# Five hand-written engine orders laid out anew, in an attention and feed-forward kernel for eight batches

## The chip, the cores and the metric

The kernel runs on one core of a Trainium2 chip. The core has a matrix engine (TensorE, PE in the rows), a vector engine (VectorE, DVE), a scalar engine (ScalarE, ACT), GpSimd (POOL) and SyncE (SP), which here only issues transfers. Each engine works through its own instructions in order, and waits on semaphores that the others and the transfers count up. The metric is the device time of one launch, in microseconds; lower is better.

## The reference

Eight batches of 512 tokens with 512 features go through two stages, each followed by a layer normalization whose result is added to the stage's input.

```python
x = x + layernorm(attn(layernorm(x)))        # 16 heads of 32, rotary positions, softmax, low-rank q and k/v (128)
x = x + layernorm(ffn(layernorm(x)))
# attn: q = rotary(c_q @ W_qr + b_qr), k = rotary(x @ W_kr + b_kr), v = c_kv @ W_uv + b_uv
#       c_q = x @ W_dq + b_dq, c_kv = x @ W_dkv + b_dkv
#       out = softmax(q k^T / sqrt(32)) v @ W_o + b_o
# ffn:  h = silu(x' @ W_gate.T * s_g) * (x' @ W_up.T * s_u);  y = fwht(h * SU_dp) @ W_down.T * s_d
#       x' = fwht(x * SU_ug); 2048 inner features
```

## The kernel before, in words

Every fp32 product is made of three fp16 products (high by high, high by low, low by high), so nearly every operand exists as a high and a low half. One batch is cut into steps, and a step is named by its kind and its number:

- `c.0`, `c.1`: the two compressions; `proj.g`: rotary inputs of head group g (4 heads of 4 groups); `v.0`, `v.1`: values. On TensorE `proj` is lines 764 and 772, `v` line 750, `c` line 738.
- `smax.g.n` (TensorE line 784, VectorE line 1326): the row maxima of group g, from scores that are made only for that; they go into `tok` (`mtok`) and then, by a transposing transfer `stq.g`, into the q stack. `stk.g.0` and `stk.g.1` (line 592) transpose the k and q stacks of group g before that; `smax.g.0` waits for both, the group's first `st` waits for `stq.g`.
- `st.U` (line 796), U = 0 to 31 in a batch, 8 for each group: one block of scores, transposed, 128 keys by 256 queries by 4 heads. ScalarE then does `exp.U` (line 1016), `exq.U` (1022) and `exr.U` (1027), VectorE `low.U` (1340, left half) and GpSimd `low.U` (1437, right half) make the low half of the probabilities `pr`.
- `av.U` (lines 812 and 817): the value product and the row sums of block U, 20 matmuls whose outputs are 32 partitions high, four of them side by side in the array. All other steps fill 128 columns of it. `pr` has two buffers, so `exp.U` waits for `av.(U-2)`; `av.U` waits for both `low.U`. After each fourth `av` a `norm.n` (VectorE, ScalarE, GpSimd) divides.
- `o.t`: output projection of 128 tokens (lines 826, 831), then normalizations `oe`, `ys`, `yn` and a transposing transfer `ln2.t` (line 570).
- `gate.i`, `up.i`, `down.i`, i = 0 to 31 (8 for each 128 tokens): the feed-forward products (lines 842, 842, 866). Between them stand `tanh.i`, `gelu.i`, `hid.i` on ScalarE, VectorE and GpSimd. `down.i` also waits for its weights, the transfer `wl.i` (line 548), which waits for `down.(i-2)`.
- `xs`, `xn`, `xl`, `ln1`: load, normalize and transpose the next batch's input. `oe.t` and `fe.t` on SP write the two results of 128 tokens; `rl` and `yl` load.

PSUM has two slots for `c`, `v`, `proj`, `smax`, `st` and `o`; the table `UPPER` says which step takes which. A step's matmuls wait for the slot's last user to be read out.

The order on each engine is written out as text, one string per engine: `FRONT` (executed once), `ORDER` (a hardware loop of six turns) and, after the loop, `ORDER` twice more with what lies beyond the last batch left out. The loop overlaps three batches: `up.4@-1` in turn b is the feed-forward step of batch b-1, `c.1@1` the one of batch b+1. `FRONT` also scales, splits and rotates the weights (`lda`, `amx`, `mx`, `ldx`, `cut`, `dy`, `dz`, `ut`, `uh`, with 56 `warm` matmuls between them to keep TensorE at work).

```python
steps(FRONT[name][skip:], FRONT_PRED)
with nc.Fori(1, NB - 1, engines=(eng.engine,), hint_back_edge=True) as b:
    steps([(b + d, s) for d, s in ORDER[name]], None)
steps(back(name), BACK_PRED)
```

Of the kernel before, what the change touches and what calls it, by code (L numbers as in the profile page):

```python
# [64 lines left out]
        smax.3.1 down.12@-1 up.15@-1 smax.3.2 c.1@1 smax.3.3 av.18 down.13@-1 av.19 st.20 c.0@1 gate.16@-1 down.14@-1
        smax.3.4 smax.3.5 up.16@-1 down.15@-1 st.21 proj.0@1 gate.17@-1 smax.3.6 up.17@-1 smax.3.7 gate.18@-1 av.20
        st.22 up.18@-1 av.21 gate.19@-1 down.16@-1 st.23 up.19@-1 down.17@-1 gate.20@-1 av.22 st.24 up.20@-1 av.23
        gate.21@-1 st.25 down.18@-1 up.21@-1 av.24 gate.22@-1 smax.0.0@1 down.19@-1 smax.0.1@1 av.25 st.26 up.22@-1
        smax.0.2@1 down.20@-1 gate.23@-1 smax.0.3@1 st.27 up.23@-1 smax.0.4@1 down.21@-1 av.26 smax.0.5@1 gate.24@-1
        av.27 st.28 proj.1@1 up.24@-1 st.29 down.22@-1 smax.0.6@1 gate.25@-1 av.28 smax.0.7@1 up.25@-1 st.30 av.29  # L70
        st.31 gate.26@-1 down.23@-1 up.26@-1 av.30 gate.27@-1 av.31 up.27@-1 v.0@1 gate.28@-1 st.0@1 down.24@-1
        up.28@-1 v.1@1 gate.29@-1 st.1@1 down.25@-1 o.0 av.0@1 down.26@-1 smax.1.0@1 av.1@1 up.29@-1 smax.1.1@1 st.2@1
        gate.30@-1 o.1 down.27@-1 smax.1.2@1 up.30@-1 av.2@1 gate.31@-1 st.3@1 o.2 down.28@-1 up.31@-1 smax.1.3@1
        down.29@-1 st.4@1 av.3@1 o.3 down.30@-1 smax.1.4@1 gate.0 down.31@-1 smax.1.5@1 proj.2@1 up.0 st.5@1 gate.1
# [5 lines left out]
        tanh.8@-1 exr.12 xn.0@1 hid.7@-1 exp.13 exq.13 tanh.9@-1 xn.1@1 exr.13 tk.3.0 norm.2 yl.1@-1 hid.8@-1 exp.14  # L80
        exq.14 hid.9@-1 fe.0@-1 tanh.10@-1 exr.14 tk.3.1 exp.15 tanh.11@-1 exq.15 hid.10@-1 exp.16 exr.15 xn.2@1
        exq.16 exr.16 hid.11@-1 exp.17 tanh.12@-1 exq.17 exr.17 hid.12@-1 xn.3@1 tanh.13@-1 exp.18 exq.18 exr.18
        exp.19 exq.19 hid.13@-1 exr.19 tanh.14@-1 hid.14@-1 c.1@1 norm.3 tanh.15@-1 exp.20 hid.15@-1 exq.20 c.0@1
        exr.20 tanh.16@-1 exp.21 hid.16@-1 exq.21 exr.21 tanh.17@-1 tk.0.0@1 exp.22 norm.4 fe.1@-1 tanh.18@-1
        hid.17@-1 exq.22 exr.22 exp.23 hid.18@-1 tanh.19@-1 exq.23 tk.0.1@1 exr.23 hid.19@-1 exp.24 exq.24 tanh.20@-1
        exr.24 exp.25 exq.25 fo.0@-1 exr.25 tanh.21@-1 hid.20@-1 exp.26 hid.21@-1 exq.26 tanh.22@-1 exr.26 norm.5
        exp.27 exq.27 hid.22@-1 exr.27 tanh.23@-1 hid.23@-1 yl.2@-1 exp.28 exq.28 exr.28 tanh.24@-1 exp.29 exq.29
        hid.24@-1 exr.29 norm.6 tanh.25@-1 exp.30 exq.30 exp.31 exr.30 exq.31 exr.31 hid.25@-1 tk.1.0@1 tanh.26@-1
        tanh.27@-1 fe.2@-1 v.0@1 exp.0@1 tk.1.1@1 exq.0@1 exr.0@1 v.1@1 norm.7 hid.26@-1 exp.1@1 exq.1@1 exr.1@1
        tanh.28@-1 oe.0 hid.27@-1 hid.28@-1 tanh.29@-1 exp.2@1 exq.2@1 exr.2@1 yn.0 oe.1 tanh.30@-1 exp.3@1 hid.29@-1  # L90
        exq.3@1 exr.3@1 oe.2 hid.30@-1 tanh.31@-1 exp.4@1 yl.3@-1 exq.4@1 hid.31@-1 exr.4@1 yn.1 oe.3 norm.0@1 fe.3@-1
        tanh.0 exp.5@1 exq.5@1 yn.2 exr.5@1 tanh.1 hid.0 tk.2.0@1 hid.1 exp.6@1 exq.6@1 exr.6@1 exp.7@1 exq.7@1 tanh.2
        yn.3 exr.7@1
# [1420 lines left out]
```

## Time and profile before

| | |
|---|---|
| Time, median of 3 runs | 1991.81 us (1990.1 to 1992.1) |
| Profiled execution: span | 2000.3 us |
| Profiled execution: its own time | given only as its span |
| TensorE busy | 1888.1 us (94%) |
| VectorE, ScalarE, GpSimd busy | 1239.4, 1094.4, 936.6 us (62%, 55%, 47%) |
| Mean granted TensorE clock | 0.987 |
| Moved by DMA | 280.95 MB, mean 140 GB/s |

TensorE's busy time is modelled from its instructions, so 94% is not 94% of its best. More is read from the distance between the start of one step and the start of the next: that distance is what the step costs on TensorE, everything included.

### The profile page before, as it was taken

The numbers are of one execution on the slowest core, as the hardware profiler recorded it, in microseconds if no ns is written. First come the engines' busy times: TensorE is split into PE (matmuls) and PEld (weight loads), VectorE is DVE, ScalarE is ACT, GpSimd is POOL, SyncE is SP. The second block draws the span as 40 slices with busy tenths as digits, with TensorE's granted clock in tenths as the row PEclk, the third lists the DMA queues.
The fourth block names the chain that finished last, engine by engine and source line by source line (L and its number), as shares of the span: only waits on it lengthen the run. The fifth ranks groups of instructions, "written<-read, shape, count | busy, mean of one in ns | idle before, by whom it ended". The sixth has DMA issues, their size and how long they took to land.

```text
span 2000.3 us, 59639 instructions
## 1 busy us (share of the span) xinstructions
PE 1888.1 (94%) x24392; PEld 1370.4 (69%) x24392; DVE 1239.4 (62%) x2141; ACT 1094.4 (55%) x1731; POOL 936.6 (47%) x958
## 2 busy tenths in 40 slices
...
GB/s 228 257 96 180 63 99 57 165 154 123 117 159 163 119 118 143 159 161 110 140 178 159 112 125 148 172 114 125 143 162 161 108 144 153 128 112 113 169 137 144
DMA packets 353029, 280.95 MB, mean 140 GB/s; under 512 B 285216, under 2 KB 286496, under 8 KB 351776
## 3 DMA queue, kind: packets, MB, share of 16 engines
...
q8 instruction: 200, 3.28, 0.7%
...
## 4 chain that ended last, share of the span: by engine, by line
PE 79%; DMA 6%; DVE 5%; SPq 4%; issue 3%; ACT 2%; POOL 1%; POOLq 0%; ACTq 0%; DVEq 0%
PE ps L842 30%; PE ps L866 15%; PE ps L784 6%; PE ps L772 5%; PE ps L796 5%; PE ps L812 5%; PE ps L831 4%; SPq L592 3%; DMA qT<-tok 2%; PE ps L817 2%; PE ps L686 2%; PE ps L738 2%; DMA room<-down_mid 1%; DVE mx L1326 1%; PE ps L674 1%
## 5 line engine op out<-in xcount | busy, mean ns | idle before, releaser
L1437 POOL TENSOR_TENSOR pr<-p,pr 128x512 f16<-128x512 f32 x256 | 298.5, 1166 | 403.5 <-ACT p L1022 403.4
L1016 ACT ACTIVATE pr<-ps,exp_scale 128x1024 f16<-128x1024 f32 x256 | 285.2, 1114 | 277.9 <-PE ps L796 256.8
L1326 DVE TENSOR_REDUCE mx<-ps 128x2 f32<-128x1024 f32 x256 | 311.9, 1224 | 160.5 <-PE ps L784 158.8
L842 PE MATMUL ps<-x2T,gate_w 128*128 128x128 f16 x6144 | 388.5, 220 | 8.1 <-issue 3.4
L842 PEld LDWEIGHTS ps<-x2T,gate_w 128*128 128x128 f16 x6144 | 359.4, 98 | 51.6 <-issue 21.0
L842 PE MATMUL ps<-x2T,up_w 128*128 128x128 f16 x6144 | 388.9, 220 | 1.9 <-issue 1.9
L842 PEld LDWEIGHTS ps<-x2T,up_w 128*128 128x128 f16 x6144 | 363.9, 98 | 37.5 <-issue 8.7
L866 PE MATMUL ps<-room 128*128 128x512 f16 x1536 | 375.7, 381 | 11.3 <-DMA room<-down_mid 11.2
L1465 POOL TENSOR_TENSOR room<-room 128x256 f16<-128x256 f32 x256 | 171.9, 676 | 252.4 <-ACT room L1052 252.3
L1340 DVE TENSOR_TENSOR pr<-ps,pr 128x512 f16<-128x512 f32 x256 | 175.7, 686 | 167.4 <-ACT ps L1027 167.2
L866 PEld LDWEIGHTS ps<-room 128*128 128x128 f16 x1536 | 142.5, 98 | 157.0 <-issue 21.1
L1047 ACT ACTIVATE room<-ps,half_gate 128x256 f32<-128x256 f32 x256 | 121.5, 474 | 227.6 <-PE ps L842 226.3
L1371 DVE SCALAR_TENSOR_TENSOR room<-room,ps 128x256 f32<-128x256 f32 x256 | 106.2, 415 | 144.1 <-ACT room L1047 144.0
L784 PE MATMUL ps<-kT,qT 96*128 96x512 f16 x512 | 154.7, 385 | 22.2 <-DMA qT<-tok 9.4
L1022 ACT ACTIVATE p<-ps,exp_scale 128x512 f32<-128x512 f32 x256 | 175.6, 686 | 0.0
L1027 ACT ACTIVATE ps<-ps,exp_scale 128x512 f32<-128x512 f32 x256 | 170.4, 666 | 0.0
L1052 ACT ACTIVATE room<-room 128x256 f16<-128x256 f32 x256 | 105.5, 415 | 116.8 <-DVE room L1373 65.3
L796 PE MATMUL ps<-qT,kT 128*128 128x256 f16 x1024 | 154.7, 274 | 5.0 <-DVE pr L1340 2.9
L1345 DVE RECIPROCAL nsc<-ps 128x256 f32<-128x256 f32 x64 | 112.4, 1756 | 64.2 <-PE ps L817 61.8
L812 PE MATMUL ps<-pr,v 128*32 128x256 f16 x3072 | 131.7, 277 | 0.5 <-POOL pr L1437 0.4
L796 PEld LDWEIGHTS ps<-qT,kT 128*128 128x128 f16 x1024 | 90.0, 98 | 48.1 <-issue 16.8
L1411 POOL TENSOR_TENSOR rs<-ve,mhalf 128x1 f32<-128x1 f32 x128 | 71.6, 564 | 106.8 <-DVE ve L1282 93.1
...
## 6 DMA issues: line engine op xcount, KB each, us to landing
room<-down_mid SPq DMA_DIRECT2D x256, 512.0 KB, 3.6
...
```

The lines of the kernel that those rows point to most:

```text
L784: mm = nc.tensor.matmul(work[k][:, i, :], qT[0:STACK, g % 2, t, h, :], kT[0:STACK, g % 2, :, h, :], start=True, stop=True)
L796: mm = nc.tensor.matmul(work[k][:, j, hh * HALF:(hh + 1) * HALF], kT[:, g % 2, kt, 2 * j + hh, :], qT[:, g % 2, 2 * qh:2 * qh + 2, 2 * j + ...
L812: nc.tensor.matmul(o_acc[h * DH:(h + 1) * DH, :], v[:, kt, pv, head:head + DH], pr[:, U % 2, pp, h, :], start=kt == 0 and i == 0, stop=Tru ...
L842: mm = nc.tensor.matmul(ffn_ps[i % 2][:, col:col + P], weights[:, chunks[j // 4], kt, pw, j % 4 * P:(j % 4 + 1) * P], x2T[:, px, kt, t * P ...
L866: mm = nc.tensor.matmul(down_ps, hid[:, i % 2, ph, jx * P:(jx + 1) * P], wr[:, i % 2, jx, pw, :], start=jj == jx == n == 0, stop=jj == NJ ...
L1016: nc.scalar.activation(pr[:, U % 2, 0].rearrange("p (j h) q -> p j (h q)", j=2), work[k], ACT.Exp, scale=exp_scale[:, 0:1]).then_inc(p_hi. ...
L1022: nc.scalar.activation(p32[:], work[k][:, 1, :], ACT.Exp, scale=exp_scale[:, 0:1]).then_inc(p_right.sem, 1)
L1027: nc.scalar.activation(work[k][:, 0, :], work[k][:, 0, :], ACT.Exp, scale=exp_scale[:, 0:1]).then_inc(p_left.sem, 1)
L1326: nc.vector.tensor_reduce(mx[:, 2 * tp:2 * tp + 2, h], work[k], AX.X, ALU.max).then_inc(sm_freed.sem, 1)
L1340: nc.vector.tensor_tensor(lo, work[k][:, 0, :], hi, ALU.subtract).then_inc(st_freed.sem, 1)
L1437: nc.gpsimd.tensor_tensor(lo, p32[:], hi, ALU.subtract).then_inc(p_low.sem, 1)
L1465: nc.gpsimd.tensor_tensor(hid[:, i % 2, 1, :], act[:, i % 2, :], hid[:, i % 2, 0, :], ALU.subtract).then_inc(h_lo.sem, 1)
```

## The change

All five strings of `ORDER` and of `FRONT` are written anew. The steps, their waits and `UPPER` are the same. Three things change:

1. In the loop's string for TensorE, `av` steps that stood alone now stand in pairs, `av.U av.(U+1)`: 14 pairs in each turn, and 8, 11, 12 and 15 alone. Before, none stood beside another. In the whole program 107 `av` steps follow directly on another one after the change (14 in the front, 84 in the loop, 9 behind it); before there were 4, all in the front. `gate`, `up`, `down` and `smax` steps also gather more in runs.
2. The loop begins elsewhere: on TensorE at `up.11@-1` instead of `av.7`, on ScalarE at `exq.10` instead of `tanh.3@-1`, on VectorE, GpSimd and SP at `xs.0@1`, `low.8` and `xl.0@1`. The front issues what comes before that, the back what comes after it.
3. On SP the transfers of the first stage's result move: `oe.3` and `ln2.3` go from before the turn's end to behind `stk.0.1@1` in the next turn, `ln2.2` goes behind `wl.6`, and `ln2.1` stands between `wl.2` and `stk.2.0@1`. In the front `ln1.0` no longer stands before `lda.5`, `ldx.0` and `lda.0`, and VectorE does `init` before `xs.0`.

The diff, cut to TensorE's and SP's loop strings and the first lines of the front:

```diff
 ORDER = dict(
     PE="""
-        av.7 gate.4@-1 st.8 up.4@-1 down.2@-1 st.9 gate.5@-1 av.8 st.10 up.5@-1 down.3@-1 gate.6@-1 smax.2.0 up.6@-1
-        smax.2.1 av.9 smax.2.2 down.4@-1 smax.2.3 st.11 gate.7@-1 smax.2.4 av.10 up.7@-1 smax.2.5 gate.8@-1 st.12
-        up.8@-1 proj.3 down.5@-1 smax.2.6 gate.9@-1 smax.2.7 av.11 down.6@-1 st.13 up.9@-1 st.14 down.7@-1 gate.10@-1
-        av.12 up.10@-1 av.13 gate.11@-1 st.15 up.11@-1 down.8@-1 st.16 av.14 gate.12@-1 down.9@-1 up.12@-1 av.15 st.17
...
-        smax.1.6@1 up.1 av.4@1 gate.2 smax.1.7@1 st.6@1 up.2 av.5@1 st.7@1 gate.3 down.0 up.3 av.6@1 down.1
+        up.11@-1 st.16 av.13 av.14 down.8@-1 down.9@-1 gate.12@-1 up.12@-1 gate.13@-1 st.17 av.15 down.10@-1
+        down.11@-1 smax.3.0 up.13@-1 av.16 av.17 st.18 st.19 gate.14@-1 up.14@-1 gate.15@-1 smax.3.1 down.12@-1
+        up.15@-1 smax.3.2 c.1@1 smax.3.3 av.18 av.19 down.13@-1 st.20 c.0@1 gate.16@-1 down.14@-1 smax.3.4
...
+        gate.0 smax.1.5@1 proj.2@1 st.5@1 up.0 gate.1 up.1 smax.1.6@1 smax.1.7@1 gate.2 up.2 av.4@1 av.5@1
+        st.6@1 st.7@1 gate.3 down.0 up.3 down.1 st.8@1 av.6@1 av.7@1 st.9@1 gate.4 up.4 gate.5 up.5 st.10@1
+        av.8@1 down.2 down.3 gate.6 smax.2.0@1 smax.2.1@1 up.6 gate.7 smax.2.2@1 smax.2.3@1 up.7 down.4
+        smax.2.4@1 st.11@1 av.9@1 av.10@1 smax.2.5@1 gate.8 down.5 up.8 st.12@1 proj.3@1 av.11@1 smax.2.6@1
+        gate.9 up.9 smax.2.7@1 down.6 st.13@1 st.14@1 gate.10 down.7 av.12@1 up.10 gate.11 st.15@1
     """,
...
     SP="""
-        xl.0@1 wl.3@-1 stk.2.1 wl.4@-1 wl.5@-1 xl.1@1 wl.6@-1 rl.0 wl.7@-1 ln1.0@1 xl.2@1 stq.2 wl.8@-1 ln1.1@1
...
-        wl.25@-1 stk.1.0@1 wl.26@-1 stk.1.1@1 wl.27@-1 rl.1 wl.28@-1 fe.1@-1 oe.0 wl.29@-1 rl.2 fe.2@-1 wl.30@-1 oe.1
-        ln2.0 wl.31@-1 wl.0 oe.2 rl.3 ln2.1 ln2.2 fe.3@-1 wl.1 stq.1@1 wl.2 stk.2.0@1 oe.3 ln2.3
+        xl.0@1 xl.1@1 stk.2.1 wl.4@-1 wl.5@-1 wl.6@-1 ln2.2@-1 wl.7@-1 ln1.0@1 stq.2 wl.8@-1 wl.9@-1 xl.2@1
+        ln1.1@1 xl.3@1 stk.3.0 wl.10@-1 wl.11@-1 stk.3.1 ln1.2@1 wl.12@-1 wl.13@-1 ln1.3@1 wl.14@-1 wl.15@-1
+        wl.16@-1 wl.17@-1 stq.3 wl.18@-1 wl.19@-1 stk.0.0@1 stk.0.1@1 oe.3@-1 ln2.3@-1 rl.0 wl.20@-1 wl.21@-1
+        wl.22@-1 wl.23@-1 wl.24@-1 wl.25@-1 stq.0@1 stk.1.0@1 rl.1 stk.1.1@1 wl.26@-1 wl.27@-1 wl.28@-1 fe.1@-1
+        wl.29@-1 oe.0 wl.30@-1 rl.2 oe.1 ln2.0 wl.31@-1 oe.2 rl.3 fe.2@-1 wl.0 wl.1 stq.1@1 wl.2 ln2.1 stk.2.0@1
+        wl.3 fe.3@-1
     """,
 )
...
 FRONT = dict(
...
     DVE="""
-        xs.0 xs.1 xs.2 xs.3 init xn.0 xn.1 xn.2 amx.4 amx.3 amx.1 abias amx.2 amx.0 mx.0 adiag.0 xs.0@1 xn.3 asc amx.5
+        init xs.0 xs.1 xs.2 xs.3 xn.0 xn.1 xn.2 xn.3 amx.4 amx.3 amx.1 abias amx.2 amx.0 mx.0 adiag.0 asc amx.5
...
     SP="""
-        xl.0 xl.1 xl.2 xl.3 lda.4 lda.2 ldv.2 lda.3 lda.1 ln1.0 lda.5 ldx.0 ldv.0 lda.0 ldx.1 xl.0@1 ln1.1 ldx.2 ln1.2
+        lda.4 xl.0 xl.1 xl.2 lda.2 xl.3 ldv.2 lda.3 lda.1 lda.5 ldx.0 ldv.0 lda.0 ldx.1 ln1.0 xl.0@1 ln1.1 ln1.2
```

ScalarE's string near the end of a turn reads after the change `... tanh.0 tanh.1 yn.1 fe.3@-1 tk.2.0@1 hid.0 hid.1 exp.6@1 exq.6@1 exr.6@1 norm.0@1 exp.7@1 exq.7@1 exr.7@1 tk.2.1@1 ...`, and GpSimd's `... hid.1 yn.1 low.6@1 low.7@1 tok.2.0@1 tok.2.1@1 norm.0@1 hid.2 oe.3`.

## Rows read from the trace of the kernel before

**Rows 1.** Windows: us, busy us per engine, PE clock, DMA share, GB/s

```profile
15.00:22.50 7.50, 0.00 (x0) 0.00 (x0) 3.43 (x8) 2.54 (x3) 4.33 (x6) 1.00 0.45 100
...
200.00:250.00 50.00, 44.78 (x452) 25.41 (x449) 32.64 (x35) 43.64 (x54) 21.90 (x14) 0.97 0.28 63
...
372.30:590.50 218.20, 215.93 (x2897) 159.57 (x2896) 141.99 (x246) 120.90 (x200) 111.18 (x119) 0.99 0.58 141
...
1461.50:1677.20 215.70, 214.19 (x2901) 159.07 (x2904) 140.51 (x244) 119.57 (x197) 109.22 (x117) 1.00 0.58 143
1677.20:1876.00 198.80, 185.51 (x2474) 140.28 (x2474) 96.74 (x186) 90.61 (x158) 79.77 (x92) 0.97 0.48 128
```

**Rows 2.** TensorE's timeline in turn 3: start us, length us, what

```profile
999.99 0.39 PE L826 MATMUL ps<-bias_o,pick_q 128*128 128x512 f16 x1
...
1002.80 1.46 PE L866 MATMUL ps<-room 128*128 128x512 f16 x6
1004.10 0.60 PE L784 MATMUL ps<-kT,qT 96*128 96x512 f16 x2
...
1007.61 0.38 PE L764 MATMUL ps<-bias_qk,pick_k 128*128 128x512 f16 x1
...
1011.39 1.50 PE L842 MATMUL ps<-x2T,up_w 128*128 128x128 f16 x24
1012.73 0.60 PE L796 MATMUL ps<-qT,kT 128*128 128x256 f16 x4
1013.16 1.50 PE L842 MATMUL ps<-x2T,gate_w 128*128 128x128 f16 x24
1014.50 0.60 PE L784 MATMUL ps<-kT,qT 96*128 96x512 f16 x2
1014.94 1.50 PE L842 MATMUL ps<-x2T,up_w 128*128 128x128 f16 x24
1016.37 0.51 PE L812 MATMUL ps<-pr,v 128*32 128x256 f16 x12
...
1017.03 1.51 PE L842 MATMUL ps<-x2T,gate_w 128*128 128x128 f16 x24
```

**Rows 3.** TensorE's timeline in the front, two value products together

```profile
165.17 0.60 PE L784 MATMUL ps<-kT,qT 96*128 96x512 f16 x2
165.70 0.51 PE L812 MATMUL ps<-pr,v 128*32 128x256 f16 x12
...
166.25 0.50 PE L812 MATMUL ps<-pr,v 128*32 128x256 f16 x12
```

**Rows 4.** TensorE's timeline: the first loop turn's start, and the loop's exit

```profile
372.32 0.51 PE L812 MATMUL ps<-pr,v 128*32 128x256 f16 x12
...
1677.17 0.51 PE L812 MATMUL ps<-pr,v 128*32 128x256 f16 x12
...
1681.53 2.20 PE L842 MATMUL ps<-x2T,gate_w 128*128 128x128 f16 x22 [3.41 <-issue]
```

**Rows 5.** Waits of TensorE from 372.3 to 1677.2: us, times, longest

```profile
PE ps L866 <- DMA room<-down_mid: 8.5, 5, 2.6
PE ps L784 <- DMA qT<-tok: 4.0, 5, 2.2
```

**Rows 6.** SP's timeline at the head of turn 4

```profile
1028.89 0.51 SPq L609 DMA_DIRECT2D y_mid<-xr  x1
1029.66 1.74 SPq L570 DMA_TRANSPOSE x2T<-nhl  x1
...
1033.35 5.60 SPq L592 DMA_TRANSPOSE qT<-tok  x1
```

**Rows 7.** The chain that ended last, at the same place: start us, us

```profile
1033.35 9.19 DMA qT<-tok
```

**Rows 8.** Groups by line and form: count, busy us, mean ns, idle before

```profile
L1437 POOL TENSOR_TENSOR pr<-p,pr 128x512 f16<-128x512 f32 x256 | 298.5, 1166 | 403.5 <-ACT p L1022 403.4
L1016 ACT ACTIVATE pr<-ps,exp_scale 128x1024 f16<-128x1024 f32 x256 | 285.2, 1114 | 277.9 <-PE ps L796 256.8 <-PE ps L817 19.7
...
L1022 ACT ACTIVATE p<-ps,exp_scale 128x512 f32<-128x512 f32 x256 | 175.6, 686 | 0.0
```

More of the change, by code:

```diff
@@ L65 @@
[L65 to L74, printed above, removed]
@@ L80 @@
[L80 to L89, printed above, removed]
@@ L90 @@
[L90 to L93, printed above, removed]
+        exq.10 exr.10 norm.1 hid.4@-1 yn.2@-1 tanh.5@-1 tanh.6@-1 hid.5@-1 hid.6@-1 exp.11 exq.11 exr.11
+        tanh.7@-1 exp.12 tanh.8@-1 exq.12 exr.12 yl.1@-1 yn.3@-1 xn.0@1 hid.7@-1 tk.3.0 hid.8@-1 exp.13
@@ new lines @@
+        tanh.9@-1 xn.1@1 exq.13 exr.13 hid.9@-1 exp.14 exq.14 exr.14 tk.3.1 fe.0@-1 tanh.10@-1 tanh.11@-1 norm.2
+        exp.15 exq.15 exp.16 exr.15 xn.2@1 exq.16 exr.16 hid.10@-1 hid.11@-1 tanh.12@-1 exp.17 exq.17 exr.17
+        hid.12@-1 tanh.13@-1 xn.3@1 exp.18 exq.18 exr.18 norm.3 exp.19 exq.19 hid.13@-1 exr.19 tanh.14@-1 c.1@1
+        hid.14@-1 tanh.15@-1 exp.20 exq.20 exr.20 hid.15@-1 c.0@1 exp.21 exq.21 exr.21 tanh.16@-1 fe.1@-1
+        hid.16@-1 norm.4 tk.0.0@1 tanh.17@-1 tanh.18@-1 hid.17@-1 exp.22 exq.22 exr.22 exp.23 exq.23 tanh.19@-1
@@ new lines @@
+        tk.0.1@1 exr.23 hid.18@-1 tanh.20@-1 hid.19@-1 exp.24 exq.24 exr.24 hid.20@-1 exp.25 fo.0@-1 exq.25
+        exr.25 tanh.21@-1 exp.26 exq.26 exr.26 hid.21@-1 tanh.22@-1 exp.27 norm.5 hid.22@-1 exq.27 exr.27 exp.28
+        exq.28 exr.28 tanh.23@-1 tanh.24@-1 hid.23@-1 exp.29 exq.29 exr.29 tanh.25@-1 norm.6 hid.24@-1 hid.25@-1
+        exp.30 exq.30 exp.31 exr.30 exq.31 exr.31 yl.2@-1 fe.2@-1 tanh.26@-1 tanh.27@-1 tk.1.0@1 tk.1.1@1 v.0@1
+        norm.7 exp.0@1 exq.0@1 hid.26@-1 hid.27@-1 v.1@1 exr.0@1 exp.1@1 exq.1@1 exr.1@1 tanh.28@-1 oe.0 exp.2@1
@@ L94 @@
+        exq.2@1 exr.2@1 tanh.29@-1 hid.28@-1 hid.29@-1 tanh.30@-1 oe.1 yn.0 exp.3@1 exq.3@1 exr.3@1 hid.30@-1
+        yl.3@-1 tanh.31@-1 oe.2 exp.4@1 exq.4@1 exr.4@1 hid.31@-1 oe.3 exp.5@1 exq.5@1 exr.5@1 tanh.0 tanh.1
+        yn.1 fe.3@-1 tk.2.0@1 hid.0 hid.1 exp.6@1 exq.6@1 exr.6@1 norm.0@1 exp.7@1 exq.7@1 exr.7@1 tk.2.1@1
+        tanh.2 tanh.3 yl.0 hid.2 exp.8@1 tanh.4 exq.8@1 exr.8@1 hid.3 exp.9@1 exq.9@1 exp.10@1 exr.9@1
     """,
     DVE="""
-        gelu.2@-1 norm.1 gelu.3@-1 low.8 xs.0@1 gelu.4@-1 low.9 gelu.5@-1 low.10 smax.2.0 smax.2.1 smax.2.2 smax.2.3
```

204 lines of the change are left out of this document (110 added, 94 removed).

## The prediction

> **What bounds the kernel now.** I read the windows first, turn by turn, to see which engine is full. In a loop turn TensorE is busy 214 to 216 us of 216 to 219, VectorE 142, ScalarE 121, GpSimd 111 [rows 1]. So TensorE's own string is the path, and the other four matter only where they make it wait. Then I read TensorE's timeline by the distance from one step's start to the next one's. The reader is to see in [rows 2] that these distances are constants: `gate` 1013.16 to 1014.50 = 1.34 (`up` the same), `smax` 0.44, `st` 0.43, `down` 1.30, `proj` 1007.61 to 1011.39 = 3.78, `o` 999.99 to 1002.80 = 2.81. For `c` (12 matmuls of 512 columns, as in `o` without its first) I take 2.59, for `v` (6 of them, as `down`) 1.30. The exception is what stands around `av`. An `up` before a score block takes 1.34, an `up` before an `av` 1014.94 to 1016.37 = 1.43: 0.09 more. The `av` itself takes 1016.37 to 1017.03 = 0.66.
>
> The 64 `gate` and `up`, 32 `down`, 32 `av`, 32 `smax`, 32 `st`, 4 `o`, 4 `proj`, 2 `c` and 2 `v` of a turn add up to 85.8 + 41.4 + 24.1 + 13.9 + 14.0 + 11.2 + 15.1 + 5.2 + 2.6 = 213.3 us. Six turns take 1677.17 - 372.32 = 1304.9 us [rows 4], 217.5 each. So 4.1 us of a turn are waits, 24.7 in the loop, and 12.5 of these have a name: `down` waits 8.5 us for its weights, `smax` 4.0 us for the transposed stacks [rows 5]. Third, I read SP's timeline where they fall, to see why the transfers are late: SP is issuing one transfer after another.
>
> **The change, part by part.** *The pairs.* The front of the kernel before already holds four pairs, and one of them shows the price. `smax` before the pair takes 165.17 to 165.70 = 0.53, which is 0.44 plus the 0.09 for coming to `av`; the first `av` then takes 165.70 to 166.25 = 0.55 instead of 0.66 [rows 3]. (The other three measure the same.) So an `av` that follows an `av` is spared 0.09 on its way in and the one before it 0.11 on its way out: 0.20 us for each new neighbourhood. There are 107 afterwards, 4 before: 103 x 0.198 = 20.4 us, 14 x 0.198 = 2.8 of it in each turn. This is on TensorE, the path itself, and nothing hides it.
>
> The Trainium skill ("TensorEngine Tiling (Array Packing)", Key Properties) says that changing the tiling mode drains TensorE, and "TensorE: Matmul & The Clock Gate", Single matmul latency, puts the fixed part of a single warm matmul at 166 ns. If each of the 206 mode changes taken away were worth that, the estimate would be 34 us and not 20.4. The trace's rows disagree in size: 0.09 in and 0.11 out.
>
> Where TensorE isn't the bound the gain goes to a wait. That is the front from 200 to 250 us, where ScalarE is busy 43.6 of 50 us [rows 1]. Six of the new pairs stand in the front ahead of 300 us; I count all six as lost, +1.2.
>
> *Later values for the pairs.* `pr` has two buffers, and a pair holds both until it runs. What is late next is `exp`. A pair needs, from its first score block on, `exp` 1.11, `exq` 0.69, `exr`, the next `exp` 1.11, `exq` 0.69 and GpSimd's `low` 1.17 [rows 8]. With `exr` as long as `exq` that is 5.5 us, against 210.6/16 = 13.2 us from one pair to the next. I went through all pairs by the constants of [rows 2]. The thinnest is `st.6 st.7 gate.3 down.0 up.3 down.1 st.8 av.6 av.7`: from the end of `st.6` to `av.7` TensorE has 0.44 + 1.34 + 1.30 + 1.34 + 1.30 + 0.44 + 0.09 + 0.55 = 6.8 us. ScalarE has `norm.0` between as well, and with it as long as `exq` the chain is 6.2 us. It fits by 0.6 us, without the semaphores between the engines. For this and places like it I add 0.4 us a turn, +2.4; the bounds are 0 and all of the 2.8 us that a turn gains, +16.8.
>
> *The transfers at the turn's end.* Before, `oe.3` and `ln2.3` stand between `stk.2.0` and `stk.2.1`; from 1028.89 to 1031.40 SP issues these two [rows 6], and `stk.2.1`, issued at 1033.35, lands 9.19 us later, at 1042.54, and `smax.2.0` begins then [rows 7]. After, both are gone from there by a hundred us; `ln2.1` comes in ahead of `stk.2.0`, `fe.3` and `xl.1` ahead of `stk.2.1`. One transposing transfer less (1.74 us of issue) and three plain ones moved about: the queue is a little shorter, not empty. `stk.2.0` stays in front of `wl.3`, and `down.3` has 10.0 us after `down.1` instead of 9.4, `smax.2.0` 22.8 after `smax.1.7` instead of 21.1 by my constants. Behind SP's transposes are queued `wl.3`, `stk.2.1`, `wl.4`, and for them wait `down.3`, `smax.2.0`, `down.4`. Bounds: all 12.5 us of [rows 5] gone, or none. I take half, -6.2. The moved `ln2.2` and `ln2.3` are wanted by `gate.16` and `gate.24`, by the constants over 100 us after `o.2` and `o.3`, so a later place costs nothing; without that cover it would be a landing each.
>
> *The turn's border.* Before, the six turns' borders show nothing on TensorE, and leaving the loop costs 3.41 us of "issue" [rows 4], and what the other engines lose there lies under it. After, TensorE leaves later than the others by some five score blocks. It pays the 3.4 us once again; the others' own pauses may now show besides: bounds 0 and 3.4 us, I take 0, since `av` has mostly over 3 us of slack. The front and the back take over steps of the loop at the same constants.
>
> *The front's start.* SP waits at `ln1.0` and the DMA share falls to 0.45 between 15.0 and 22.5 us, where 1.00 was to be had [rows 1]; afterwards `lda.5`, `ldx.0` and `lda.0` are ahead of that wait, and VectorE's `init` lies before the first tile's landing. At most 7.5 x 0.55 = 4.1 us; at least 0, because VectorE's and the transfers' later work stays the same. I take half, -2.0.
>
> **Sum.** -20.4 + 1.2 + 2.4 - 6.2 - 2.0 = -25.0 us against the profiled execution's span of 2000.3, which is 8.5 us over the median of the runs: 1975.3 there, 1991.8 - 25.0 = 1966.8 in the runs. I say 1967 us, with its own range from 1960 to 1975.
>
> **Rivals.** (1) *The pairs pay and nearly all known waits go as well.* If the 12.5 us at the turn's head vanish, the front gives 4.1, no new wait comes: -20.4 - 12.5 - 4.1 = -37, 1955 us. For it speaks that the waits are all at one place, which the change relieves; against, that `stk.2.0` still precedes `wl.3`. The drain of 34 us falls here too: if leaving and entering `av` cost more among full-width steps than [rows 3] shows, the time would be 1953. I give that alone 0.02, since three numbers of [rows 2, 3] speak against it.
>
> (2) *Part of the gain becomes waits.* The thin places cost 2 us a turn, 12, and SP's queue gives nothing: -20.4 + 1.2 + 12 = -7 to -15, 1977 to 1987 us. For it: five orders were written at once, and each misjudged wait comes six times. Against: slack per `av` by the constants is mostly 3 to 9 us, as before.
>
> (3) *Nothing to be measured.* As (2), with 3 to 4 us a turn.
>
> (4) *Slower: ScalarE stands before `exp.6`.* In its string `yn.1`, `fe.3`, `tk.2.0`, `hid.0` and `hid.1` now stand ahead of it. `yn.1` hangs on a chain through all engines, `fe.3` on `down.31`. If one is late, `exp.6` is, then `av.6`, `av.7`, `st.8` and all behind. It decides when it costs over 25/6 = 4.2 us a turn; at 6 us a turn the kernel takes 1967 + 36 = 2003 us. Against it: from `down.31` to `st.6` TensorE has 1.34 + 0.44 + 3.78 + 0.43 + 4.02 + 0.87 + 2.68 + 1.31 + 0.44, over 15 us.
>
> **How the numbers follow.** The forecast (1960 to 1975) 0.50, rival 1 0.20, rival 2 (1975 to 1988) 0.19, rival 3 0.04, rival 4 0.07. A measurement of this kernel tells 0.2%, 4 us, from no change. Faster: 0.50 + 0.20 + 0.19 = 0.89; same 0.04; slower 0.07. The range leaves out rivals 3 and 4, the slower end of 2, and the outer part of 1: 1954 to 1983.
>
> **What would show it.** A turn of about 213.5 us instead of 217.5, its steps adding up to 210.6; `av` to `av` 0.55 us; waits of TensorE for `down_mid` and `qT` in the loop near 6 us instead of 12.5; VectorE's and ScalarE's busy time unchanged and TensorE's down by some 20 us in span. In the front the DMA share from 15.0 to 22.5 us should be near 1 instead of 0.45. The prediction is wrong if `av` pairs cost 0.66 each in the loop, if a new wait of more than 1 us stands in every turn (first suspects `av.7`, `smax.2.0`, `down.3`), or if the loop's exit costs several pauses one after another.

## The result, and the profile after

| | before | after |
|---|---|---|
| median of 7 runs | 1992.12 us (1990.1 to 2001.63) | 1983.22 us (1974.87 to 1986.47) |
| ratio, 95% interval | | 0.9939 [0.9918, 0.9961] |
| span of the profiled execution | 2000.3 us | 1973.0 us |

The change makes the kernel faster, by 12 us by the ratio (9 by the medians) where 25 were forecast; 1983.2 lies above the forecast's own range, 1960 to 1975, and a hair above the whole range on record, 1954 to 1983. The profiled execution of the kernel after was the fastest of its seven and that of the kernel before was slow for its kind, so the two spans differ by 27.3 us, twice what the runs do. A second profile of each (the first two runs below) has spans of 1981.6 and 1993.5 us, and is set beside the first where sums are compared.

The windows of the kernel after; the first answers to the first of [rows 1], the others are one turn and all six turns of the loop:

```profile
15.00:22.50 7.50, 0.00 (x0) 0.00 (x0) 7.42 (x17) 2.43 (x3) 3.13 (x3) 1.00 1.00 324
...
1063.79:1280.96 217.17, 211.45 (x2899) 160.36 (x2896) 141.40 (x245) 118.58 (x197) 108.93 (x117) 1.00 0.57 142
416.55:1712.62 1296.07, 1268.41 (x17379) 961.51 (x17376) 843.64 (x1455) 709.71 (x1175) 650.24 (x694) 1.00 0.57 142
```

A turn takes 1296.07/6 = 216.0 us. TensorE's busy time in one fell from 215.1 us to 211.4, but the turn only from 217.5 to 216.0: what the steps lost in length came back as gaps. In the second profiles the turn even grew, from 216.6 to 217.4 us. TensorE's timeline at the start of turn 4 shows both the gain and the largest gap (compare `av` in [rows 2, 3]; an `av` is the two rows L825 and L830):

```profile
1063.79 1.50 PE L855 MATMUL ps<-x2T,up_w 128*128 128x128 f16 x24
1065.13 0.60 PE L809 MATMUL ps<-qT,kT 128*128 128x256 f16 x4
1065.66 0.51 PE L825 MATMUL ps<-pr,v 128*32 128x256 f16 x12
...
1066.22 0.50 PE L825 MATMUL ps<-pr,v 128*32 128x256 f16 x12
1066.55 0.39 PE L830 MATMUL ps<-pr,ones 128*32 128x256 f16 x7
1068.67 0.28 PE L830 MATMUL ps<-pr,ones 128*32 128x256 f16 x1 [1.74 <-issue]
1068.98 2.33 PE L879 MATMUL ps<-room 128*128 128x512 f16 x10
```

The pair is there at its forecast price (1065.66 to 1066.22 = 0.56). And in the middle of one `av`, before its last matmul, TensorE stands still for 1.74 us: no semaphore, no buffer, only "issue". After the loop's border 24 + 4 + 20 + 19 = 67 matmuls run without a break, and the 68th is late; it is the 68th in each of turns 2 to 6. The waits of TensorE over the loop (what waits, for what: us, times, longest), which answer to [rows 5], and below them a third line that the kernel before has besides the two of [rows 5]:

```profile
PE ps L797 <- DMA qT<-tok: 12.9, 8, 2.6
PE ps L830 <- issue: 9.8, 5, 2.6
PE ps L825 <- DVE nsc L1359: 2.2, 5, 0.4
PE ps L809 <- ACT ot L1054: 2.0, 6, 0.3
PE ps L879 <- DMA room<-down_mid: 0.3, 1, 0.3
```

```profile
PE ps L842 <- issue: 1.9, 4, 1.0
```

The weights' wait is gone (8.5 to 0.3), the stacks' wait has taken its place (4.0 to 12.9), and the border's pause, which the kernel before has too, has grown from 1.9 to 9.8. SP's timeline at the head of turn 4, and from the chain that ended last its DMA piece there, which answer to [rows 6, 7]:

```profile
1018.93 3.26 SPq L605 DMA_TRANSPOSE kT<-tok  x1
1022.31 0.51 SPq L561 DMA_DIRECT2D room<-down_mid  x1
1022.92 0.37 SPq L626 DMA_DIRECT2D out<-room  x1
1024.04 0.88 SPq L570 DMA_DIRECT2D xa<-in_x  x2
1025.27 3.55 SPq L605 DMA_TRANSPOSE qT<-tok  x1
```

```profile
1025.27 7.09 DMA qT<-tok
```

These are `stk.2.0`, `wl.3`, `fe.3`, `xl.0` and `xl.1`, `stk.2.1`, and then the time from the issue of `stk.2.1` to its landing. The stack of `smax.2.0` lands at 1032.36, and `smax.2.0` starts at 1032.41.

To compare whole executions I took, for every step of TensorE, its distance to the next step. The sum of the constants of [rows 2, 3] is the floor; what the distances have over it is waits, the half-clock stretches included. The floor is thus computed and not measured; what tests it stands under the pairs, behind the experiments.

| us | first step | floor | waits: front | loop | back and tail |
|---|---|---|---|---|---|
| before | 32.3 | 1844.0 | 67.1 | 24.7 | 23.9 |
| before, second profile | 31.7 | 1844.0 | 63.7 | 19.6 | 26.4 |
| after | 27.9 | 1823.6 | 74.7 | 32.6 | 6.0 |
| after, second profile | 26.5 | 1823.6 | 74.1 | 41.0 | 8.2 |

In means of the two: -4.8 at the start, -20.4 in the floor, +9.0 in the front, +14.7 in the loop, -18.1 at the end, -19.6 in all. Without what came at the end the change would have gained 1.5 us by these profiles.

### The profile page after: what moved, and what is told of

Its sections match the earlier page's. It is cut to its first block, busy times and chain, and to the rows that moved or that the text cites. A ratio compares the mean times of both kernels' runs of the same rounds, so it can differ in the third digit from the quotient of the medians.

```text
span 1973.0 us, 59664 instructions
## 1 busy us (share of the span) xinstructions
PE 1859.2 (94%) x24392; PEld 1376.0 (70%) x24392; DVE 1238.5 (63%) x2141; ACT 1086.6 (55%) x1731; POOL 935.1 (47%) x958
## 4 chain that ended last, share of the span: by engine, by line
PE 43%; issue 24%; POOL 15%; DVE 6%; DMA 6%; ACT 3%; SPq 3%; POOLq 0%; DVEq 0%; ACTq 0%
PE ps L855 15%; PE ps L879 7%; POOL pr L1450 4%; DMA qT<-tok 4%; PE ps L797 3%; POOL room L1478 3%; PE ps L699 3%; PE ps L809 3%; PE ps L825 2%; PE ps L785 2%; PE ps L751 2%; DVE mx L1339 2%; POOL tok L1444 2%; POOL rs L1424 1%; PE ps L830 1%
## 5 line engine op out<-in xcount | busy, mean ns | idle before, releaser
L855 PEld LDWEIGHTS ps<-x2T,up_w 128*128 128x128 f16 x6144 | 358.1, 98 | 23.5 <-issue 1.7
L879 PE MATMUL ps<-room 128*128 128x512 f16 x1536 | 365.6, 379 | 1.8 <-POOL room L1478 1.0
L797 PE MATMUL ps<-kT,qT 96*128 96x512 f16 x512 | 149.7, 385 | 29.8 <-DMA qT<-tok 21.7
L809 PE MATMUL ps<-qT,kT 128*128 128x256 f16 x1024 | 148.7, 274 | 12.7 <-DMA qT<-tok 6.1
L825 PE MATMUL ps<-pr,v 128*32 128x256 f16 x3072 | 130.1, 275 | 2.2 <-DVE nsc L1359 2.2
L809 PEld LDWEIGHTS ps<-qT,kT 128*128 128x128 f16 x1024 | 92.4, 98 | 52.7 <-issue 15.2
```

Of the source, the lines that this page charges most:

```text
L797: mm = nc.tensor.matmul(work[k][:, i, :], qT[0:STACK, g % 2, t, h, :], kT[0:STACK, g % 2, :, h, :], start=True, stop=True)
L809: mm = nc.tensor.matmul(work[k][:, j, hh * HALF:(hh + 1) * HALF], kT[:, g % 2, kt, 2 * j + hh, :], qT[:, g % 2, 2 * qh:2 * qh + 2, 2 * j + ...
L825: nc.tensor.matmul(o_acc[h * DH:(h + 1) * DH, :], v[:, kt, pv, head:head + DH], pr[:, U % 2, pp, h, :], start=kt == 0 and i == 0, stop=Tru ...
L855: mm = nc.tensor.matmul(ffn_ps[i % 2][:, col:col + P], weights[:, chunks[j // 4], kt, pw, j % 4 * P:(j % 4 + 1) * P], x2T[:, px, kt, t * P ...
L879: mm = nc.tensor.matmul(down_ps, hid[:, i % 2, ph, jx * P:(jx + 1) * P], wr[:, i % 2, jx, pw, :], start=jj == jx == n == 0, stop=jj == NJ ...
```

## The experiments

Each was timed against the kernel before on its own chip; a comparison of two changed kernels goes by their ratios, times 1996 us. The interval of such a difference is 6 to 7 us to either side (5 where a kernel was measured twice), so that 12 and 22 us are clear of it, 7 barely, and 2 and 5 are not.

**Both kernels again.** No edit.

> The changed kernel once more, unchanged, as the baseline of this call and for a second profile. Theory: the pairs save 20.4 us on TensorE for certain, and waits at three fixed places of each loop turn (a pause of TensorE after 67 matmuls of the turn, the wait of smax.2.0 for its stack, av.12) plus two in the front give some of it back; so the turn's waits again sum to 3 to 7 us, the same steps named. Rival: the give-back is the chance of one execution, and the places differ in a second profile. Time about 0.994 of the kernel before.

> The kernel before, unchanged, for a second profile. The profile before had waits of 20 us behind the loop against 4.5 in the changed kernel's, and its span was some 8 us over the median. If that was one execution's chance, a second profile has a span of 1990 to 1993 and 8 us less of waits, most of it behind the loop; if the waits behind the loop belong to the order, they are within 3 us of 24 again and the 8 us are missing elsewhere.

After: 1983.48 us (1979.12 to 1985.94), ratio 0.9929 [0.9902, 0.9957]; before 1995.36. The mean of the two ratios, 0.9934, is the kernel after in what follows. The waits behind the loop of the kernel before are 26.4 us in its second profile, 23.9 in its first: they belong to its order and not to one execution. In the kernel after the loop's waits were 41.0 us here and 32.6 in the first profile, that is 6.8 and 5.4 a turn, at the same steps; much of the difference comes from seven stretches of 3.4 us, six in the loop and one at its exit, in which the granted clock is 0.50 (1.2 GHz), each behind a pause after the border or a wait for the stacks. The first profile has none in the loop. One of them, in windows (the granted clock is the number 0.50 behind the brackets):

```profile
1033.20:1036.60 3.40, 3.40 (x36) 3.40 (x34) 2.45 (x3) 0.78 (x2) 0.02 (x1) 0.50 0.03 13
```

**The border moved.** Kernel after; TensorE's loop starts at `down.2`, 35 of its 204 steps earlier; the order of the steps is the same, but for `gate.6`, which the front had once before `down.2`.

```
ORDER PE: -   up.11@-1 st.16 av.13 av.14 down.8@-1 ... av.8@1 down.2 down.3 gate.6 ... st.15@1
          +   down.2@-1 down.3@-1 gate.6@-1 ... st.15 up.11@-1 st.16 av.13 av.14 ... av.8@1
```

> The changed kernel with only TensorE's border moved: its loop turn begins at down.2 instead of up.11, the execution order of all steps stays (but for gate.6 before down.2 once in the front). Theory: after the border TensorE has about 65 matmuls at hand and the rest comes 4 to 6 us later; from up.11 with its pair of av those last 3.0 us, from down.2 on 6.2 us, so the pause of 1 to 2.6 us in turns 2 to 6 (11.6 us in all in the profile) goes, and the time falls by 9 to 12 us against a_again, 0.5% to 0.6%. Rival 1: the pause comes from a busy DMA, and at down.2, where the stacks are transposed, it is as long or longer: no gain, or 2 to 5 us lost. Rival 2: what TensorE gains there it waits for at smax.3.0 and smax.2.0: gain under 4 us.

Measured 1969.34 us, ratio 0.9868 [0.9839, 0.9896]; the same kernel again in a later comparison 1968.93, 0.9877 [0.9852, 0.9901]. That is 13 and 11 us less than the kernel after by the ratios, 12 in the mean (14 by the first medians). Its waits over the loop:

```profile
PE ps L796 <- DMA qT<-tok: 8.0, 6, 1.7
PE ps L878 <- issue: 5.5, 1, 5.5
```

The five pauses are gone, the stacks' wait is down from 12 or 13 us to 8 (9.2 in the second profile), and the pause at the loop's exit is 5.5 us (6.0) where the kernel after has 2.0.

**The pairs taken apart.** Kernel after; the second `av` of each pair goes behind the next step.

```
ORDER PE: -   st.16 av.13 av.14 down.8@-1 ...
          +   st.16 av.13 down.8@-1 av.14 ...   (and 104 more)
```

> The changed kernel with every pair of value products taken apart by one step (the second av goes behind the step that followed it, at proj the first goes ahead of the step before it); all else stays. 105 of the 107 neighbourhoods go. Theory: 105 x 0.198 = 20.8 us slower than a_again by the steps' cost alone, less what waits that now overlap hide, so 14 to 21 us, 0.7% to 1.05%. Rival: the waits set the loop's pace (stacks, border), and the pairs are covered by them: under 8 us slower.

1991.5 us, 0.9966 [0.9949, 0.9984]: against the kernel after in the same comparison 7 us slower by the ratios and 8.0 by the medians, outside the theory's 14 to 21. But the loop's head, the first steps behind the border, became looser by this edit too: the pauses, here from start to start, fell from 11.9 to 4.9 us. This run can't tell a small value of the pairs from a border that hides it. The next one is free of the pauses:

**The pairs taken apart, border at `down.2`.** Both edits, and its partner without the split.

> The kernel of a_border again, unchanged (kernel after with TensorE's border at down.2), as the partner of a_bsplit on the same chip: 1966 to 1972 us, as in the first comparison (1969.3).

> The kernel of a_border2 with all pairs taken apart: the second av of each goes behind the next step that is no av. What the pairs are worth by themselves, where no pause after the border can take part of it. Theory (0.198 us for each of 104 neighbourhoods, all on the path; the 8.0 us that a_split cost in place of 20.8 were short because the looser head shortened the border's pause by 7 and the other waits by 5): 15 to 21 us slower than a_border2, some 1986. Rival (half of the pairs' gain is always given back in other waits, wherever the border is): 6 to 11 us slower, some 1978.

1993.42 against 1968.93 us, ratios 0.9993 [0.9972, 1.0014] against 0.9877: +23 us, a little over the expected 15 to 21 and three times the rival's 6 to 11. In the two profiles, which lie 28.6 us apart, the floor rises by 20.8 and the waits by 7.9. So the pairs' price reaches the end in full; that taking them apart adds waits besides isn't told from the spread of executions. The same run shows what the rest of the new orders is worth together, without pairs and without the pauses: nothing that can be told, 1 us with an interval of 4 to either side. In its profile the earlier start and the shorter tail are there and are eaten up by longer waits in the front and the loop.

**`stk.2.1` earlier.** Kernel after; SP's queue alone.

```
ORDER SP: -   xl.0@1 xl.1@1 stk.2.1 wl.4@-1 ... ln2.1 stk.2.0@1 wl.3 fe.3@-1
          +   xl.0@1 xl.1@1 wl.4@-1 ... ln2.1 stk.2.0@1 wl.3 stk.2.1@1 fe.3@-1
```

> Kernel after; on SP's queue alone stk.2.1 moved from the turn's start to the turn before, right behind stk.2.0 and wl.3, so that it no longer stands behind wl.3, fe.3, the border and both xl transfers. Theory (the wait of 1.9 us a turn of smax.2.0 is SP's place for stk.2.1): the 11 to 12 us of that wait fall to under 3, TensorE's half-clock stretches that follow it fall with it, -8 to -11 us against the kernel after, some 1974. Rival (the transposing transfer, not its place, is the bound): it lands as late, or down.4 and down.5 wait for wl.4 and wl.5 instead, under -3 us. Prediction on record put this whole term at -6.2 and thought half of it gone.

1974.44 us, 0.9899 [0.9873, 0.9925]: -7 us by the ratios, just short of the expected 8 to 11 (-9.0 by the medians, from two chips). Its waits over the loop:

```profile
PE ps L830 <- issue: 11.2, 5, 2.7
PE ps L855 <- DVE room L1386: 4.1, 5, 1.3
...
PE ps L797 <- DMA qT<-tok: 1.9, 2, 1.2
```

The stack's wait fell from 12 to 1.9, and a wait of `gate.7` for VectorE took 4.1 of it back; the border's pause stayed.

**`stq.0` earlier in the front.** Kernel after.

```
FRONT SP: -   ldx.10 ldx.11 rl.0 rl.1 stq.0 stk.1.0
          +   ldx.10 stq.0 ldx.11 rl.0 rl.1 stk.1.0
```

> Kernel after; in the front, on SP's queue alone, stq.0 moved ahead of ldx.11, rl.0 and rl.1 (loads of 1.5 MB). Theory (proj to smax.0.0 and dy.1 to st.0 wait 10 us more than in the kernel before because stq.0 lands 9.4 us after its issue instead of 4.3): the first st comes 4 to 7 us earlier and the end with it, -4 to -7 us. Rival (front bound by VectorE and ScalarE, whose strings also have xn.0 of the second batch ahead of smax.0.7 now): the first st comes earlier but a later wait in the front takes it back, under -2 us at the end.

1980.13 us, 0.9923 [0.9898, 0.9948]: 2 us less by the ratios, which isn't told from nothing; the theory's 4 to 7 didn't come. `stq.0` lands 4.3 us after its issue instead of 9.4, the wait of `st.0` falls from 7.3 to 2.1 us, but that of `st.1` is then 4.6: `exp.0` and what follows it had been hidden behind the transfer. The wait before `smax.0.0`, 7.9 and 8.8 us in the two profiles of after and 4.9 and 6.4 in those of before, stays at 8.8; no run went after it.

**All three.** Border, `stk.2.1` and `stq.0`.

> Kernel after with three edits: TensorE's border moved to down.2 (as in the run a_border), stk.2.1 earlier (as in a_stk), stq.0 earlier (as in a_stq). If the three causes are separate, the gains add: -14 (a_border, measured) -9 -5 = -28 us against the kernel after, some 1955; if the border pause and the stack wait cover one another, -18 to -22, some 1963.

1960.66 us, 0.9825 [0.9797, 0.9853]: 22 us less than the kernel after. The parts measured one by one are 12, 7 and 2: they add up. Expected were 28 us of separate causes, by the medians of the single runs, or 18 to 22 of causes that cover one another; with parts as small as these against their intervals the run can't tell the two apart.

**The front amended once more.** As before it, and:

```
FRONT SP:  -   dst.6 raw.5 raw.6 ln1.0@1 dst.7 dst.8      +   dst.6 ln1.0@1 raw.5 dst.7 dst.8 raw.6
FRONT DVE: -   xn.0@1 mx.8 mx.9 smax.0.7 mtok.0           +   smax.0.7 mtok.0 xn.0@1 mx.8 mx.9
```

> The kernel of a_all with the front amended once more: raw.5 and raw.6 (2 MB) behind ln1.0 of the second batch on SP's queue, and smax.0.7 and mtok.0 ahead of xn.0 of the second batch, mx.8 and mx.9 on VectorE. Theory (dy.2 to st.1 +4.7 and dz.9 to st.13 +4.5 us come from these): the front 4 to 8 us shorter, some 1955 us. Rival (the front between 130 and 200 us is bound by VectorE and ScalarE in sum, so a wait taken away comes back): within 2 us of a_all.

1959.21 us, 0.9813 [0.9787, 0.984]: within 2.4 us of the last one, not told from it; the expected 4 to 8 didn't come. The wait of 4.5 us before `st.13` is gone, that before `st.0` is back at 3.3, that of `st.1` stays at 4.6. It is the fastest kernel of the study, 1.9% under the kernel before and 1.2% under the kernel after.

**The mirror: the kernel before with the border at `up.11`.**

```
ORDER PE: -   av.7 gate.4@-1 ... gate.11@-1 st.15 up.11@-1 down.8@-1 st.16 av.14 ... down.1
          +   up.11@-1 down.8@-1 st.16 av.14 ... down.1 av.7@1 gate.4 ... gate.11 st.15@1
```

> The kernel before with one edit, the mirror of a_border: TensorE's loop border alone moved from av.7 to up.11, the place it has in the kernel after. Theory (the pause after the back edge shows in full only where no other wait lies in the first three to five us after the border; at av.7 it lies mostly under the waits of down.2 and down.3 for their weights): a pause of 1.5 to 2.5 us appears near the 65th matmul in turns 2 to 6, +5 to +10 us in the loop; leaving the loop gets cheaper by 0 to 4 us, so +2 to +10 us in all. Rival (the pauses belong to the pairs or to the new orders of the other engines, not to the border's place): no pause, within 2 us of the kernel before.

2001.32 us, 1.0024 [1.0004, 1.0044]; +5 us. The time is inside the expected range, the reason is not: there is no pause in the loop. TensorE's timeline behind the border of turn 4:

```profile
1066.34 1.50 PE L849 MATMUL ps<-x2T,up_w 128*128 128x128 f16 x24
1067.68 1.46 PE L873 MATMUL ps<-room 128*128 128x512 f16 x6
1068.97 0.60 PE L803 MATMUL ps<-qT,kT 128*128 128x256 f16 x4
1069.50 0.51 PE L819 MATMUL ps<-pr,v 128*32 128x256 f16 x12
```

So the border's place alone doesn't do it. But here `down.8` stands before the `av`, and the 68th matmul begins 4.6 us after the border, in the kernel after it could begin after 2.9. That gave the next two runs. What makes this kernel slower (its waits sum to 114.1 us, between those of the two profiles of before) wasn't found.

**The mirror with one pair in the head.** As the last one, and (the bar stands for the border):

```
ORDER PE: -   up.10 av.13@1 gate.11 st.15@1 | up.11@-1 down.8@-1 st.16 av.14 gate.12@-1
          +   up.10 gate.11 st.15@1 | up.11@-1 st.16 av.13 av.14 down.8@-1 gate.12@-1
```

> The kernel before with TensorE's border at up.11 (as in the run b_border, which showed no pause) and, right behind it, the one pair av.13 av.14 ahead of down.8, as in the kernel after; nothing else paired. Theory: the 66 matmuls last 2.9 us instead of 4.5, and a pause comes back; since b_border's 4.5 us were always enough, it can be at most 1.6 us a turn if the instructions come as there, 1.3 to 2.9 if they come as in the kernel after. Against b_border the loop gets 0 to +7 us slower (a neighbourhood gives 0.2 a turn back). Rival (the pause in the kernel after is due to what SP transfers at that moment, not to the dense head): no pause here, within 2 us of b_border.

```profile
1067.11 1.50 PE L848 MATMUL ps<-x2T,up_w 128*128 128x128 f16 x24
...
1070.21 0.39 PE L823 MATMUL ps<-pr,ones 128*32 128x256 f16 x7
1071.45 0.28 PE L823 MATMUL ps<-pr,ones 128*32 128x256 f16 x1 [0.85 <-issue]
```

One pair brings the pause back, at the same 68th matmul, in turns 2 to 6. That matmul begins 4.1 to 4.3 us after the border; in the kernel after 4.1 to 5.8. The time, 2003.71 us, 1.0048 [1.0021, 1.0075], is 5 us over the mirror's with overlapping intervals; the profile has 4.0 us of pauses.

**The head loosened.** Kernel after, border unmoved.

```
ORDER PE: -   up.11@-1 st.16 av.13 av.14 down.8@-1 down.9@-1 gate.12@-1
          +   up.11@-1 st.16 down.8@-1 down.9@-1 av.13 av.14 gate.12@-1
```

> Kernel after; on TensorE alone, right behind the unmoved border, down.8 and down.9 are put ahead of the pair av.13 av.14 (up.11 st.16 down.8 down.9 av.13 av.14 instead of up.11 st.16 av.13 av.14 down.8 down.9). Theory: the instructions after the back edge reach TensorE 4 to 6 us after it, whatever it does; the 66 matmuls that it already has last 2.9 us with the pair in front, some 4.1 with the two down in front, so the pause of 1.3 to 2.9 us a turn falls to 0 to 1.5, 1.2 us less a turn, -6 to -10 us in all (with fewer half-clock stretches behind them). Rival (the pause belongs to the border's place in the whole order, or to the length of the loop's code): it stays at 1.3 to 2.9 us, within 2 us of the kernel after.

1977.78 us, 0.9908 [0.9883, 0.9934], -5 us by the ratios, with overlapping intervals, where 6 to 10 were expected. What is plain is the profile: the pause is gone in all turns, the stacks' wait stays, and a new wait came, for a buffer that is late by now:

```profile
PE ps L798 <- DMA qT<-tok: 11.0, 6, 2.3
PE ps L880 <- POOL room L1479: 7.5, 6, 1.2
```

`down.10` now waits 1.2 us a turn for GpSimd's `hid`, so 7.5 of the 10 us came back.

**SP's big transfer away from the border.** Kernel after.

```
ORDER SP: -   ln1.1@1 xl.3@1 stk.3.0 wl.10@-1 wl.11@-1 stk.3.1
          +   ln1.1@1 wl.10@-1 wl.11@-1 xl.3@1 stk.3.0 stk.3.1
```

> Kernel after; on SP's queue alone xl.3 and stk.3.0 moved behind wl.10 and wl.11, so that the big transposing transfer (5.1 us of issue) is no longer issued 0.9 us after TensorE's back edge but some 8 us after it. Theory 2 (the instructions of the loop's head come over the same DMA engines as the data and wait there: 4.1 to 5.8 us in the kernel after at a DMA share of 1.18, under 4.4 in b_border at 0.67): the pause before the 67th matmul falls from 1.3 to 2.9 us to under 1.5. Theory 1 alone (fixed time): it stays as it is. In both, smax.3.0 waits 2 to 5 us a turn longer for its stacks, so the whole time says nothing and is +0 to +20 us; the pause is what is read.

2025.52 us, 1.0148 [1.0119, 1.0178]. Its waits over the loop:

```profile
PE ps L855 <- DVE room L1386: 30.7, 6, 6.0
...
PE ps L830 <- issue: 9.2, 5, 2.1
```

The pauses are 1.9 to 2.3 us each instead of 1.3 to 2.9, 9.2 in sum instead of 9.8, not under 1.5 as the second theory had it. That clears this one transfer and not the transfers as such: around the border the DMA share is 0.98 here (863.5 to 869 us), 1.13 and 1.01 in the kernel after, so others took its place. The 43 us are a misjudgement of mine. It isn't `smax.3.0` that waits for the late stack, it is VectorE that waits for the late `xl.3` (9.6 us at its `xs.3`), and behind it in VectorE's string stands `gelu.11`, whose buffer `gate.13` needs.

**What comes before a pause ends.** No edit: the DMA packets in the profiles of the kernels above. Besides the data the profile has packets of the kind "instruction". The kernel after has 200 of 16,384 bytes on one queue, 23 or 24 in each turn, and one begins 1.5 to 3.2 us after each back edge. (That they are TensorE's instructions is read from what follows.) In the lines, number of packets, MB and share of the engines' time; the first is of the whole execution, the second of the 0.1 us from 1066.2 us, in turn 4:

```profile
q8 instruction: 200, 3.28, 0.7%
```

```profile
q8 instruction: 1, 0.02, 62.8%
```

In turn 4 this packet ends at 1067.24 us, 3.45 us after the border, and the 68th matmul begins at 1068.67, 1.43 us later. In us after the border, turns 2 to 6:

| kernel | the packet ends | late matmul begins | with constants alone it would begin |
|---|---|---|---|
| before, two profiles | 2.0 to 3.0 | 65th: 3.6 to 4.5 | 3.3 |
| after, two profiles | 2.6 to 4.0 | 68th: 4.1 to 5.8 | 2.9 |
| mirror | 1.9 to 2.2 | no pause | 68th: 4.6 |
| mirror with one pair | 2.6 to 2.8 | 68th: 4.1 to 4.3 | 3.2 |
| after, border at `down.2`, two profiles | 3.1 to 4.1 | no pause | 68th: over 6 |
| the same with `stk.2.1` and `stq.0` earlier | 2.1 to 2.6 | no pause | 68th: over 6 |

In all 43 pauses of the nine profiles that have them TensorE goes on 1.3 to 1.7 us after the end of this packet, and at the loop's exit 1.2 to 1.9 us after the end of one. The last two rows differ, inside the loop, in the place of `stk.2.1` alone, and with this transfer away from the border the packet ends more than 1 us earlier.

## Why the forecast was half right

**The pairs, -20.4: right.** In the kernel after the distance from an `av` to an `av` is 0.556 us in the median, and 104 of the 107 lie within 0.02 us of it; an `av` before any other step still takes 0.65 to 0.66, and a step before an `av` 0.09 more than elsewhere. (That the floor falls by 20.4 and that the steps of a turn add up to 210.6 follows from the constants and tests nothing.) The pairs alone are worth 23 us in the runs (`a_bsplit`). The rule of the Trainium skill ("TensorEngine Tiling (Array Packing)", Key Properties) that a change of the tiling mode drains TensorE agrees with the trace in its sign. The estimate of 34 us, for which the prediction took the fixed part of a matmul from the Trainium skill's "TensorE: Matmul & The Clock Gate", Single matmul latency, finds no support: the size here was 0.20 us for a pair of mode changes.

**The turn's border, 0: the step that failed.** It said that the borders "show nothing on TensorE" and that only leaving the loop costs. The first was not so even in the kernel before: in its turns 2 to 5 the 65th matmul begins 0.66, 0.40, 1.21 and 0.46 us after the 64th, where 0.06 is the rule, which I had overlooked. What the runs show in its place is this. After the back edge TensorE has 64 to 67 matmuls at hand; the next comes 3.6 to 5.8 us after the border, 1.3 to 1.7 us after the packet of instructions has come in. What is visible is that time less the time that the matmuls at hand take. In the kernel before they take 3.3 us, in the mirror 4.6, behind `down.2` over 6; in the kernel after they take 2.9, because a pair stands there, the densest steps in the kernel by matmuls (20 in 0.56 us). So the change paid with its own coin. Moving the border gives 12 us (measured twice): the pauses, 11 to 12 us from start to start, and 3 to 5 of the stacks' wait are gone, the exit takes 3.4 to 4 us more, and half-clock stretches behind the pauses go with them.

**Waits in the new orders, +2.4: near in size, by luck.** `av.12` waits 0.4 us a turn for VectorE's division (L825, `nsc`) and `st.4` 0.3 for ScalarE (L809): 4.2 us in the loop. The mechanism on record, a pair that waits for late `exp`, shows nowhere: the suspect `av.7` has no wait.

**SP's transfers, -6.2: failed, 0 came.** 12.5 us [rows 5] became 13.2 (9.6 and 12.0 in the second profiles). What I had counted as relief (`ln2.3`, `oe.3` gone) helped `down.3`; but the same sum had `fe.3`, `xl.0`, `xl.1` in front of `stk.2.1` and called the queue "a little shorter". `smax.2.0` is where I said a new wait would be looked for, at 1.9 us a turn. The bound of all 12.5 us was real: moving one token takes 10 us off this wait and gives 7 in time.

**The front, +1.2 and -2.0: right to sign, blind to what follows.** The DMA share from 15.0 to 22.5 us is 1.00 as forecast, and the first step comes 4.8 us earlier, more than the bound of 4.1. But the front's waits grow by 9.0. SP's timeline, first of after and then of before:

```profile
100.16 0.37 SPq L522 DMA_DIRECT2D x2T<-in_W_gate  x1
100.70 0.88 SPq L579 DMA_DIRECT2D xr<-in_x  x2
101.88 7.38 SPq L605 DMA_TRANSPOSE qT<-tok  x1
```

```profile
99.62 1.67 SPq L592 DMA_TRANSPOSE qT<-tok  x1
101.70 0.86 SPq L509 DMA_DIRECT2D x2T<-in_W_gate  x1
```

The same transposing transfer, issued right behind three plain loads, holds SP for 7.38 us instead of 1.67 and lands after 9.44 instead of 4.27 us. I had read the front's orders for its first 25 us and for its pairs, not for that swap. `a_stq` shows that undoing it gives some 2 us, not told from nothing, since `st.1` then waits for VectorE (`pr`) in its place; what the rest of the 9 us is was not settled (`a_best` took away one wait of 4.5 and gained nothing that can be told).

**Back and tail, 0: failed, -18 came.** TensorE's waits from the loop's exit to the end, of the kernel after, of before, and of the mirror, whose exit is where that of the kernel after is:

```profile
PE ps L855 <- issue: 2.0, 1, 2.0
PE ps L797 <- DVE mx L1339: 1.3, 1, 1.3
PE ps L879 <- POOL room L1478: 1.0, 1, 1.0
```

```profile
PE ps L842 <- issue: 3.4, 1, 3.4
PE ps L842 <- DVE room L1373: 3.4, 2, 2.7
PE ps L866 <- DMA room<-down_mid: 2.7, 3, 1.4
PE ps L784 <- DVE pr L1340: 2.3, 2, 2.0
PE ps L796 <- DVE pr L1340: 1.7, 1, 1.7
```

```profile
PE ps L873 <- DMA room<-down_mid: 3.5, 4, 1.5
PE ps L849 <- DVE room L1380: 3.4, 2, 2.7
PE ps L849 <- issue: 2.8, 1, 2.8
```

The mirror keeps the tail of before (24.6 us of waits in all), so the exit's place isn't what mended it. Nor are the pairs, since the tail stays short with them taken apart (6.5 and 7.1 us of waits in `a_split` and `a_bsplit`). Some of it is the clock: behind the loop the kernel before has three stretches of 3.4 us at 1.2 GHz in either profile, the kernel after none and one. What is left are the new orders of the back, of TensorE or of the other engines; which of them does it was not tried, and the cause of the largest single miss stays open. [Rows 1] had shown it: 185.5 us busy of 198.8 in the window behind the loop, 13 us of waits in a stretch to which I gave one sentence.

**The sum.** Against the forecast's -25: the border +12, SP's transfers +6, the front's waits +8, against them the tail -18 and the start -3. That is -20, as the profiles' means have it; the runs say -12 to -14. The difference is within what single executions of one kernel differ by (1975 to 1986 us), much of it half-clock stretches. That the kernel came out faster at all is luck by this account: the loop, the front and the start together leave 1.5 us of the pairs' 20.4, and the rest is the tail, to which the forecast gave nothing. Rival 2, that part of the gain becomes waits, is what happened, by its number if not by its place: 1977 to 1987 us were on record for it, with a chance of 0.19. (Its own terms give 1985 with all of the 12 us of waits; 1987 lies beyond them. In the same way the turn of 213.5 us under "What would show it" is 214.1 by the forecast's terms.)
